# Moving the gate and up products of a feed-forward layer into the attention beats, with their gated product kept in device memory

## What is computed

```python
xn = layernorm(x)
# attention: 16 heads of 32, q and k RMS-normed and rotated, causal
q, k, v = split(xn @ w_qkv)
s = softmax(mask(rope(rms(q)) @ rope(rms(k)).T / sqrt(32))) @ v @ w_out
# feed-forward layer, hidden size 1408, integer weights less 128, times a scale
gate = silu((xn @ (wq_gate - 128).T) * s_gate)
up = (xn @ (wq_up - 128).T) * s_up
g = silu(((gate * up) @ (wq_down - 128).T) * s_down)
out = x + s * g
```

## Time and profile before

| | |
|---|---|
| time, median of 3 executions | 803.49 us (799.95 to 803.91) |
| the profiled execution | span 804.2 us, within the spread of the three |
| TensorE matmuls, busy | 725.5 us, 90% of the span, 4160 matmuls |
| VectorE busy | 511.2 us, 64% |
| ScalarE busy | 445.4 us, 55% |
| GpSimd busy | 344.8 us, 43% |
| DMA | 65.01 MB, mean 81 GB/s |
| last P times v evacuated (end of attention) | 548.4 us |

### The profile page before, as it was taken

The page is one execution under the profiler, slowest core; times in us unless marked ns, Lnnn a source line. Parts: engine busy times, 40 slices in busy tenths (PEclk is TensorE's granted clock), DMA queues, the critical chain, the costliest instruction groups (busy, mean ns, idle before and its releaser), DMA issues.

```text
span 804.2 us, 13711 instructions
## 1 busy us (share of the span) xinstructions
PE 725.5 (90%) x4160; PEld 588.4 (73%) x4160; DVE 511.2 (64%) x985; ACT 445.4 (55%) x1007; POOL 344.8 (43%) x539
## 2 busy tenths in 40 slices
PE   3779979999998799998999999669999999999997
PEld 2668857777877677777777787347888888888885
DVE  3767888888878678878888866634434334334343
ACT  2538858878668577777787767563331331331331
POOL 6556757577656467655677655210350000000000
PEclk9979989999999899999999999858999999999999
DMA  8300011241111231120131120563474114114101
GB/s 277 140 18 15 16 34 35 68 139 35 30 59 41 70 132 33 37 61 29 34 119 36 35 74 28 126 211 105 151 235 180 57 62 148 51 74 146 41 0 52
DMA packets 34659, 65.01 MB, mean 81 GB/s; under 512 B 10016, under 2 KB 12704, under 8 KB 32544
## 3 DMA queue, kind: packets, MB, share of 16 engines
q1 hardware_dynamic: 34592, 64.19, 24.8%
HBM read 38.61 MB, written 16.91 MB: 69 GB/s over the span
## 4 chain that ended last, share of the span: by engine, by line
PE 48%; POOL 24%; issue 15%; DVE 7%; DMA 4%; ACT 1%; SPq 1%; POOLq 0%; DVEq 0%; ACTq 0%
PE bank L1132 20%; PE bank L1143 10%; POOL rb L469 8%; POOL rr L458 8%; PE bank L950 6%; POOL ra L465 5%; PE bank L1031 3%; PE bank L1012 2%; PE bank L991 2%; DMA xr<-w_gu 2%; PE bank L975 2%; DVE mx L791 2%; PE bank L962 1%; POOL on L478 1%; DVE pl L772 1%
## 5 line engine op out<-in xcount | busy, mean ns | idle before, releaser
L458 POOL TENSOR_TENSOR rr<-ss,half 128x8 f32<-128x8 f32 x64 | 106.5, 1664 | 98.3 <-DVE ss L742 98.3
L772 DVE TENSOR_TENSOR pl<-pf,ph 128x512 fp32r<-128x512 f32 (+1 forms) x192 | 126.2, 658 | 8.7 <-ACT ph L573 7.8
L791 DVE TENSOR_REDUCE mx<-bank 128x1 f32<-128x384 f32 (+3 forms) x176 | 109.0, 633 | 23.1 <-PE bank L1014 22.8
L572 ACT ACTIVATE pf<-bank 128x512 f32<-128x512 f32 (+1 forms) x192 | 100.6, 524 | 25.6 <-PE bank L991 15.0
L573 ACT ACTIVATE ph<-bank 128x512 fp32r<-128x512 f32 (+1 forms) x192 | 101.5, 529 | 0.0
L868 DVE SCALAR_TENSOR_TENSOR hf<-bank,scales,gs 128x512 f32<-128x512 f32 x44 | 33.0, 751 | 106.0 <-ACT gs L663 106.0
L469 POOL TENSOR_TENSOR rb<-qn,sg 128x64 f32<-128x64 f32 x256 | 98.9, 416 | 0.0
L1132 PE MATMUL bank<-xnt_h,wgu 128*128 128x512 f32 x352 | 94.3, 390 | 0.0
L1132 PE MATMUL bank<-xnt_l,wgu 128*128 128x512 f32 x352 | 94.1, 389 | 0.0
L991 PE MATMUL bank<-ph,va 128*65 128x512 f32 (+3 forms) x256 | 80.0, 334 | 14.6 <-DVE pl L772 9.6
L465 POOL TENSOR_TENSOR ra<-qn,cg 128x128 f32<-128x128 f32 x128 | 64.0, 521 | 63.3 <-DVE qn L749 63.3
(11 more groups left out here) (80 smaller groups left out, 1457.5 us busy)
## 6 DMA issues: line engine op xcount, KB each, us to landing
xr<-w_gu SPq DMA_DIRECT2D x11, 512.0 KB, 6.9
xr<-x SPq DMA_DIRECT2D x16, 256.0 KB, 3.7
xnt_dram<-xnt_h SPq DMA_DIRECT2D x4, 1024.0 KB, 6.3
xnt_dram<-xnt_l SPq DMA_DIRECT2D x4, 1024.0 KB, 9.6
oh<-oraw SPq DMA_DIRECT2D x64, 64.0 KB, 1.9
ol<-oraw SPq DMA_DIRECT2D x64, 64.0 KB, 2.0
rdb<-rd_dram SPq DMA_DIRECT2D x16, 256.0 KB
s_dram<-s_sb SPq DMA_DIRECT2D x16, 256.0 KB, 2.0
```

Of the source, the lines that this page charges most:

```text
L458: pool.tensor_tensor(rr[:, s, :], ss[:, s, :], half[:], ALU.pow).then_inc(rr_ok, 1)
L772: dve.tensor_tensor(pl[:, tile], pf[:, tile], ph[:, tile].bitcast(F32), ALU.subtract).then_inc(pl_ok, 1)
L791: dve.tensor_reduce(mx[:].rearrange("p (h t) -> p h t", t=TB)[:, h0:h0 + len(heads), qb], bank[:, 0:len(heads) * w].rearrange("p (h n) -> ...
```

## The change

The gate and up products leave the second part and are done inside the beats, the 22 "halves" of a batch (half 2m is gate tile m, half 2m+1 up tile m, 8 matmuls each) in twelve of its sixteen beats: beats -3 to 8 for batch 0, 13 to 24, 29 to 40 and 45 to 56 for the others, mostly two a beat. The turned x is still on chip then, so `xnt_dram` goes. Silu is done as (tanh(z/2)+1)*z with the half folded into the scales. The gated product, as float32, is stored to `hf_dram`. All beats are written out, without a loop.

The fp32r gate and up weights no longer fit; they are made once, by GpSimd in beats -4 to 7, stored to `wg_dram`, and reloaded for each later batch through a ring of four. One PSUM bank is taken from the projection for the halves: each projection now waits until the one before is fully evacuated (`vl_ok`). The down weights and batch 0's hidden tiles are loaded in beats 57 to 61; the first two down tiles run in beats 63 and 64. The rest of the down products are the second part: for batches 1 to 3 the hidden tiles come from `hf_dram` through six slots (`ins`), and ScalarE and VectorE make high and low parts (`high`, `low`) as they come.

```diff
-        QKV_PS, X_PS, W_PS, ST_PS, PV_PS = psum[0:2], psum[2:4], psum[4], psum[5:7], psum[7]
-        GU_PS, DN_PS = psum[0:4], psum[4:8]
+        QKV_PS, GU_PS, X_PS, W_PS, ST_PS, PV_PS = psum[0], psum[1], psum[2:4], psum[4], psum[5:7], psum[7]
+        DN_PS = psum[0:4]
...
+RING, INS = 4, 6
+FIRST, PER_BEAT = -3, (2, 2, 2, 2, 2, 2, 2, 2, 1, 2, 1, 2)
+CHUNKS = ((0, 1, 2), (3, 4, 5), (6, 7, 8), (9, 10))
...
 # TensorE
+            def gate_half(qq):
...
+                if b == 0:
+                    pe.wait_ge(wgc_ok, q + 1)
+                else:
+                    wait(pe, wg_in[s], 16 * len([v for v in range(HALVES, qq + 1) if v % RING == s]))
+                if q % 2:
+                    pe.wait_ge(ga_ok, n + 1)
+                else:
+                    wait(pe, hf_ok, n)
+                todo = [(x_, k) for x_ in (xnt_h, xnt_l) for k in range(KT)]
+                for a, (x_, k) in enumerate(todo):
+                    op = pe.matmul(GU_PS[:], wgu[:, s, k, :], x_[:, k, :],
+                                   start=(a == 0), stop=(a == len(todo) - 1))
...
-                    wait(pe, sq_ok, n - 1)
-                    wait(pe, vh_ok, n - 1)
-                    wait(pe, vl_ok, n - 1)
+                    wait(pe, sq_ok, n)
+                    wait(pe, vh_ok, n)
+                    wait(pe, vl_ok, n)
...
                     p_v(r, c - 1, 2)
+                gate_half(half_at(c, 0))
...
+                gate_half(half_at(c, 1))
+                if c >= DOWN_AT:
+                    down(0, c - DOWN_AT)
                 if attend:
                     p_v(r, c, 0)
...
 # ScalarE and VectorE, once per hidden tile
+                act.activation(g2[:, n % 2, :], GU_PS[:], ACT.Tanh,
+                               scale=hsc[:, 0, n % MT:n % MT + 1]).then_inc(th_gate, 1)
...
+                    dve.scalar_tensor_tensor(g2[:, n % 2, :], g2[:, n % 2, :], 1.0, GU_PS[:],
+                                             ALU.add, ALU.mult).then_inc(ga_ok, 1)
...
+                    dve.scalar_tensor_tensor(g2[:, n % 2, :], GU_PS[:], hsc[:, 1, m:m + 1], g2[:, n % 2, :],
+                                             ALU.mult, ALU.mult).then_inc(hf_ok, 1)
...
 # SP, start
             sp.dma_start(stage[:, :, G * 3 * GC:], w_out).then_inc(w_in[G], 16)
+            sp.dma_start(sgu[:, 0, :], s_gate).then_inc(sc_in, 16)
+            sp.dma_start(sgu[:, 1, :], s_up).then_inc(sc_in, 16)
...
 # GpSimd, end of tables() in beat -8
                 pool.wait_ge(tab_ok, 2 * TB * 3)
+                pool.wait_ge(sc_in, 32)
...
 # SP, second part
+            for n in range(B * TB):
+                b, t = divmod(n, TB)
+                if b + 1 < B:
+                    for m in CHUNKS[t]:
+                        load_in(stage_no(MT * (b + 1) + m))
+                if TB < n <= 2 * TB:
+                    s_store(B - 1, n - TB - 1)
+                if n:
+                    store(*divmod(n - 1, TB))
+                    if n - 1 + TB < B * TB:
...
+                        load_xs(nb, nt)
...
 # VectorE, second part
+            for n in range(B * TB):
+                b, t = divmod(n, TB)
+                if b + 1 < B:
+                    for m in CHUNKS[t]:
+                        low(MT * (b + 1) + m)
+                scaled(b, t)
+                if n:
+                    finish(*divmod(n - 1, TB))
```

## The result

The changed kernel takes 896.39 us (median of 4 runs, 894.52 to 896.89) against 803.70 us of the kernel before (799.95 to 804.31): a ratio of 1.1164, 95% interval 1.1128 to 1.1199. The forecast was 812 with a range of 782 to 842. The direction was right, the size was not: the loss is 93 us where 8 were forecast. The profiled execution's span is 892.7 us.

The account below looks back on a forecast made before the run. The prediction took TensorE as nearly gapless in the second part and beats 29 to 40, with room only in the first beats and last eight. Attention ending at 677 us plus a 135 us second part gave 812, range 782 to 842.

Parts of the forecast that it names:

- gated stretches over 130 us: Sign that the forecast is wrong: twelve-beat stretches with gate and up products exceed 130 us, TensorE waiting for their weights.
- Gated stretches, +30.6 each: Beats 13-24, 29-40, 45-56: 39.1 us of matmuls come in, 10 fill idle, 1.5 new waits; bounds 26 to 37.
- Weights come late: Rival: loads and conversions behind SyncE's reciprocal wait stall TensorE 1 to 3 us some 12 times; +25, 837 us, chance 0.11.
- Beats 0 to 8, +18: Batch 0's 16 halves add 28.4 us, 12 hidden in idle, 2 for a late conversion; bounds 14 to 26.
- The bank in ungated beats +5: Beats 9-12, 25-28, 41-44: each projection waits 0.4 us for the one before, 12 times; bounds 0 to 12.
- no loop -7: Beats 25 to 28, where the loop turned back, lose their extra over beats 9 to 12 (37.20 against 30.05 us).
- the start +5: GpSimd's tables wait for gate and up scales queued behind w_out, delaying the lead-in's chain 5 us; 0 to 6.
- the +2: Lead-in, beats -6 to -4: the projection's wait for its single bank lies on the chain, 2 us.
- Beats 57 to the end, +10: Beat 57 to attention's end: copies, subtracts and two down tiles come in, waits and conversions go; bounds 0 to 20.
- The second part, 135: Behind attention: a load, high, low, result, store loop of 9.3 us a group sets 135 us; bounds 118 to 150.
- a rival's: Rival: half clock in the second part, from matmul bursts with waits between; +25, 837 us, chance 0.12.
- The loads run ahead: Rival: in the second part SP's loop is shorter than TensorE's 4.9 us; 99 us there, 776 in all, chance 0.13.

Follow-up runs that it names:

- e1: Changed kernel with the store and load of the denominators' reciprocal one beat later in SyncE's order; 871.93 us.
- e5: Changed kernel with e1's and e2's reorderings, plus GpSimd's weight conversions ahead of the LayerNorm root and head outputs' sum and norm; 828.10 us.
- e10: e8 with one matmul instead of eight in each half of a gate or up tile; 747.75 us.
- e8: Changed kernel with the five edits of e1, e2, e5, e6 and e7 together; 818.31 us.
- e4: Changed kernel with seven of the eight matmuls of each gate or up half left out; 793.15 us.
- f1: Kernel before the change, with one PSUM bank for the qkv projection instead of two; 824.40 us.
- f2: Kernel before the change, with all its beats written out instead of two passes of a loop; 797.56 us.
- e6: Changed kernel with e1's and e2's reorderings, plus gate and up scales loaded before the second block of qkv weights; 824.94 us.
- e7: Changed kernel with e1's and e2's reorderings, plus the stored product's first high halves in beat 59 instead of 58, later loads following; 826.31 us.
- e2: Changed kernel with the second part's loads issued one group ahead, before SyncE waits to store a result; 855.54 us.
- e9: e8 with the first six product tiles of batch 1 loaded at the end of SyncE's beat 63; 807.77 us.

## Why the prediction was wrong, by its own steps

The profiled span is 81 us above the forecast of 812. In the terms of its sum 37 of them lie in the gated stretches (42.1, 43.4 and 44.0 for three times 30.6), 26 in beats 0 to 8, 14 behind attention and 4 in beats 57 to its end; the small terms together are 1 under. One of its own signs of being wrong came true: gated stretches over 130 us, with TensorE waiting for wgu.

*Gated stretches, +30.6 each.* Measured +42 to +44. The matmuls are 0.2325 us apart (0.93 us for four, 420.99 to 421.92), so 176 are 40.9 and not 39.1; 6 us were filled, not 10; the bank, put at nothing behind the cover of the halves, costs 2.3. That makes 37, and e1's 129.3 less 92.2 is 37.1 (37.9 in the third stretch). The other 5 to 6 are one late weight per stretch. This is the failing step in its first form: of the bounds 5 and 13 for what is filled I took the middle, where 5.0 was the visible idle. Of the 8 us of hidden idle behind 48 waits, 1 or 2 were there to be filled.

*Weights come late.* It was a rival at 0.11 and "once" in the sum. It is a step that failed: the count was wrong, and the price was not 1 to 3 us but 2.4 us in beat 4, 7.0 and 4.2 in beat 6, and 3.5 at the most in beats 18, 34, 50, each with slow matmuls behind it. I had named the right wait, SyncE at the next beat's reciprocal, and excused it with a ring of four. (GpSimd's order is behind the waits of 2.4 and 4.2 us, as e5 shows.) But the ring's order is that of the issue: a load cannot be two beats ahead when it stands behind a wait that ends one beat on. The price as shown by e1: 24.5 us.

*Beats 0 to 8, +18.* Measured +44.2. Of its terms the 12 us of cover come near: e10 leaves out 112 matmuls of e8, 26.0 us, and the stretch falls by 12.7, so 13 were covered; from the changed kernel to e4 it falls by 14.4, so 12 were (rough figures, since e10 has its own late transfer). 16 halves are 29.8 us where 28.4 were counted. What failed stands beside them: the bank, put at nothing, is 6.9 (f1), and the late weights, put at 2, are 10 (5.7 by e1, 4.3 by e5). That gives some 34. The cause of the last 10 stays open: in e10 every beat of the stretch is 1.4 to 2.6 us longer than before, of which the bank and the matmuls left in are about 1.2 on average, and GpSimd is busy for 66.3 of 84.4 us where it was for 42.7 of 64.7.

*The bank in ungated beats +5, no loop -7, the start +5.* 1.5 to 1.8 us in each of three stretches and 7.4 for the loop (37.2 to 29.8, f2): right. GpSimd's first root is at 21.63 us: right; e6 puts that term at 6.5, and f1 the lead-in's bank at 2.4 for the +2. Beat 0 starts 10.5 us later, 11 had been forecast.

*Beats 57 to the end, +10.* Measured +13.5, inside its bounds. The wait at the reciprocal is there again, now with the stored product's loads behind it, but e1 gained only 2.5 net, since the wait came back smaller in beat 63. e7 gained 3.2: ScalarE had stood at loads that SyncE can issue only when the last product's store has landed (store issued at 687.57, first load at 693.35, with 3.9 us of SyncE's wait between them released by that store).

*The second part, 135.* 149.2, counted from the end of attention as the forecast was. The mechanism was right, two terms were mis-sized; the 22.6 us behind the eleventh result are as forecast. The first result is stored 25.6 us after attention, not 20: the loads were there when forecast (16.8; the first highs start at +17.2), but VectorE makes the first result only behind the lows and the scaling of the next group:

```profile
765.25 1.90 DVE L901 TENSOR_TENSOR ht_l<-ins,ht_h 128x512 fp32r<-128x512 f32 x3 [1.22 <-ACT ht_h L695]
...
767.67 0.68 DVE L968 TENSOR_TENSOR res<-gt,xs 128x512 f32<-128x512 f32 x1
```

And ten turns of the loop take 101.0 us instead of 92.4, 10.1 a turn for 9.3. From the store at 769.11 to the first high at 774.71 it is 5.6 us; then the three tiles land close together, and three highs and the last low take 2.7 (to 777.38) where I counted one of each, 1.2; scale and result 1.9. The granted clock of 0.82 behind 748 us was a rival's, and did not come to its price of 25: what is over the forecast lies in the two terms above. "The loads run ahead" came true as soon as the order allowed it: 120.7 us from beat 63 in e2.

*The whole.* The premise held: work moved from a stretch where TensorE has no gap to one with few gaps. Against the kernel before, e9 pays 112 us in the gated stretches, 33 in beats 0 to 8 and 5 at the start; it gets 148 back from beat 63 on, and 3 in the rest. That is nothing either way. The other 89 us of the loss were queues and waits, with the same matmuls in all of these kernels, and those are what I under-counted. Of the six edits that took them away, e5 changes GpSimd's order; the other five change what stands ahead of what in SyncE's in-order queue (e7 also when the passes behind the loads are made).

## What to carry to other kernels

When work moves into a loop that is already full, its matmuls cost their full time less the idle that the profile shows; don't add hidden slack without a run. Then walk each in-order DMA queue past every wait that stands in it, and ask of each load behind it when it can be issued at the earliest, whatever the depth of its ring. Here a late load cost twice, once as a wait and once in slow matmuls behind it (a wait of 3.55 us, 6.2 us of beat 34); and an order that is right for long beats can be wrong for short ones (e10).

## What the runs showed of the hardware

A bank less for the projection, which looked like 0.4 us here and there, cost 2.6% (f1). The place where the loop over 16 beats turns back for its second pass cost 7.4 us, nearly one per cent, with the granted clock at 0.86 in these four beats and 1.00 without the loop. The 256 KB loads of gate and up weights took 4.1 us at the median to land in the changed kernel and 2.9 with e1's order. VectorE's 512-column subtraction L848 takes 0.68 us in most cases and 1.57 at 424.43, and its mean over 128 is 0.816 us; why some are long no run shows. Four matmuls behind a wait of 3.55 us ran at the same 2.07 us as behind one of 7.01.
